# Two LSTM layers with attention and FFN on one core: bias written by VectorE, side work in equal steps, waits of the scan exchanged

## The reference

```python
def lstm(x, h0, Wx, Wh, b):            # c0 = 0
    for t in range(128):
        a = x[:, t] @ Wx + b + h @ Wh   # 16 x 512
        i, f, o, g = sigmoid(a_i), sigmoid(a_f), sigmoid(a_o), tanh(a_g)
        c = f * c + i * g
        h = o * tanh(c)
x = x + attention(lstm(x, cond, layer 1))   # linear attention scores, no softmax, scale 1/sqrt(128)
x = x + ffn(lstm(x, cond, layer 2))         # relu(h @ W1 + b1) @ W2 + b2, width 512
```

## Time and profile before

| | |
|---|---|
| runs, median (lowest to highest) | 485.77 us (484.74 to 487.51) |
| profiled execution, its own time | 481.0 us |
| its span, first to last instruction | 479.0 us |
| mean granted TensorE clock | 0.996 of 2.4 GHz |
| TensorE products busy | 462.4 us, 97% |
| TensorE weight loads busy | 349.3 us, 73% |
| VectorE busy | 260.7 us, 54% |
| ScalarE busy | 212.1 us, 44% |
| GpSimd busy | 17.4 us, 4% |
| DMA, mean over the span | 17 GB/s |

### The profile page before, as it was taken

How to read it: one execution, slowest core, us unless ns; L and a number is a source line. 1 busy time by engine, 2 the same in 40 slices (tenths; PEclk the granted TensorE clock), 3 DMA queues, 4 the chain that set the end, 5 groups by cost and what they waited for, 6 DMA issues and landing times.

```text
span 479.0 us, 17186 instructions
## 1 busy us (share of the span) xinstructions
PE 462.4 (97%) x6440; PEld 349.3 (73%) x6440; DVE 260.7 (54%) x1422; ACT 212.1 (44%) x1092; POOL 17.4 (4%) x29
## 2 busy tenths in 40 slices
PE   7999999999999999999999999999999999999997
PEld 5777666777666777766789877777777777777775
DVE  4545555555555555555545655555555555555554
ACT  2444444544444445444435344444444444444443
POOL 6700000000000000000000000000000000000000
PEclk9989999999999999999999999999999999999999
DMA  5010111110011111010000000000000000000000
GB/s 163 8 19 2 15 16 16 16 16 12 5 16 16 16 16 16 2 15 11 11 13 3 7 19 19 16 16 16 8 8 16 16 16 16 15 1 16 16 16 11
DMA packets 11689, 8.12 MB, mean 17 GB/s; under 512 B 1097, under 2 KB 11129, under 8 KB 11674
## 3 DMA queue, kind: packets, MB, share of 16 engines
q1 hardware_dynamic: 10874, 6.17, 6.5%
q0 software_dynamic: 512, 1.22, 0.9%
q10 hardware_dynamic: 288, 0.52, 0.3%
HBM read 2.87 MB, written 1.05 MB: 8 GB/s over the span
## 4 chain that ended last, share of the span: by engine, by line
PE 88%; DVE 4%; ACT 3%; issue 3%; DMA 1%; DVEq 0%; ACTq 0%
PE fobank L387 20%; PE gibank L377 16%; PE fobank L377 13%; PE bankV L363 5%; PE gibank L352 4%; PE bankY L531 4%; PE gibank L357 4%; PE fobank L352 4%; PE bankU L524 3%; PE fobank L357 3%; DVE cell L750 2%; PE bankV L441 2%; ACT scan L665 2%; PE bankU L459 2%; PE bankU L363 2%
## 5 line engine op out<-in xcount | busy, mean ns | idle before, releaser
L387 PEld LDWEIGHTS fobank<-ring,whf 128*128 128x128 f32 x510 | 76.5, 188 | 94.7 <-DVE ring L753 94.6
L662 ACT ACTIVATE fgate<-fobank 128x16 f32<-128x16 f32 x256 | 46.9, 183 | 164.8 <-PE fobank L387 162.5
L387 PE MATMUL fobank<-ring,whf 128*128 128x16 f32 x510 | 99.5, 270 | 10.4 <-DVE ring L753 0.7
L750 DVE TENSOR_TENSOR_SCAN cell<-scan 128x48 f32<-128x48 f32 x256 | 68.8, 269 | 53.2 <-ACT scan L665 52.8
L746 DVE TENSOR_TENSOR scan<-fgate,cell 128x16 f32<-128x16 f32 x256 | 45.3, 177 | 85.6 <-ACT fgate L662 83.7
L377 PEld LDWEIGHTS gibank<-h_hi,wh_parts 128*128 128x128 bf16 x1536 | 78.8, 110 | 0.0
L753 DVE SCALAR_TENSOR_TENSOR ring<-cell,ogate 128x16 f32<-128x16 f32 x256 | 44.7, 175 | 59.9 <-ACT cell L672 59.9
L377 PE MATMUL gibank<-h_hi,wh_parts 128*128 128x16 f16 x1536 | 75.4, 169 | 0.0
L377 PE MATMUL gibank<-h_lo,wh_parts 128*128 128x16 f16 x1536 | 75.3, 169 | 0.0
L665 ACT ACTIVATE scan<-gibank 128x32 f32<-128x32 f32 x256 | 54.8, 214 | 28.2 <-PE gibank L377 0.2
L377 PE MATMUL fobank<-h_hi,wh_parts 128*128 128x16 f16 x771 | 59.9, 174 | 0.4 <-ACT fgate L662 0.4
(11 more groups left out here) (150 smaller groups left out, 467.1 us busy)
## 6 DMA issues: line engine op xcount, KB each, us to landing
rows_t<-rows SPq DMA_DIRECT2D x16, 128.0 KB
x_rows<-in_x_dram SPq DMA_DIRECT2D x17, 64.0 KB
out_dram<-y_sb SPq DMA_DIRECT2D x16, 64.0 KB
xres<-x2T SPq DMA_DIRECT2D x15, 64.0 KB, 1.9
xin<-x2T SPq DMA_DIRECT2D x14, 64.0 KB, 1.8
w<-in_L_ffn_W_dram POOLq DMA_DIRECT2D x2, 256.0 KB, 3.9
wh<-in_L_cond_Wh_dram ACTq DMA_DIRECT2D x1, 256.0 KB, 2.8
wx<-in_L_cond_Wx_dram ACTq DMA_DIRECT2D x1, 256.0 KB, 3.9
```

The lines of the kernel that those rows point to most:

```text
L387: nc.tensor.matmul(step_out(p, t, GF), whf[layer][:], ring[:, (s - 1) % STEPS, :], start=False, stop=True, skip_group_check=True).then_inc ...
L662: nc.scalar.activation(fgate[:], fobank[p][:, NB * t:NB * t + NB], ACT.Sigmoid).then_inc(f_done[layer], 1)
L750: nc.vector.tensor_tensor_scan(out=c_scan, data0=scan_mul, data1=scan_add, initial=0.0, op0=ALU.mult, op1=ALU.add).then_inc(c_ready[layer], 1)
```

## The change

Six things:

1. The scan's two waits change places, and the f*c wait counts n + 1 instead of n + 2: the clearing of c has a semaphore of its own, waited for once per layer.
2. The bias matrices become 128 x 4 tiles, loaded element by element by two DMAs each (384 and 128 elements). `bias_gate` and the tile of ones are gone. VectorE writes the bias into the banks instead, by two broadcast copies of 256 elements per chunk, `seed_gi` and `seed_fo`; TensorE waits for both ahead of the chunk's first projection.
3. The copies stand behind steps t = 1, 2 (layer 1), t = 0, 1 (layer 2's loop), and together behind steps 1 and 11 of layer 2's first iteration, at the start, and between the layers.
4. Layer 1's row products move from t = 0 to t = 1; its projections from t = 2, 3 (one, three) to t = 3, 5 (two each). In layer 2's first iteration the four projections of step 12 move to 13, 14, 15 (one, one, two).
5. `WARM1` and `WARM2` are raised, and in layer 1 the filling passes go to `bankV` with a weight tile of zeros that adds to the bank, since it holds the early attention's sums.
6. The first four warming passes open the four gate banks instead.

```diff
-    WARM1 = [0, 0, 0, 0, 1, 3, 1, 3]
-    WARM2 = [1, 1, 0, 1, 1, 1, 1, 1]
+    WARM1 = [2, 1, 1, 1, 1, 1, 1, 3]
+    WARM2 = [1, 1, 1, 2, 1, 1, 2, 2]
...
-        bias = [sb(f"bias{n}", [P, 4 * H]) for n in (1, 2)]
+        bias = [sb(f"bias{n}", [P, 4]) for n in (1, 2)]
...
-            nc.vector.memset(c_psum, 0.0).then_inc(fc_done[layer], 1)
+            nc.vector.memset(c_psum, 0.0).then_inc(c_cleared, 1)
+            nc.vector.wait_ge(c_cleared, layer + 1)
+        def load_bias(eng, layer, b, done):
+            eng.dma_start(bias[layer][:, 1:4], b[0:3 * H].rearrange("(g p) -> p g", p=P),
+                          allow_slow_non_contiguous=True).then_inc(done, 16)
+            eng.dma_start(bias[layer][:, 0:1], b[3 * H:4 * H].unsqueeze(1),
+                          allow_slow_non_contiguous=True).then_inc(done, 16)
...
             sp.dma_start(x_rows[:, 0, :], x_ctb[0]).then_inc(rows_loaded[0], 16)
-            sp.wait_ge(bias1_cleared, 1)
-            sp.dma_start(bias[0][0:1, :], l1_b.unsqueeze(0)).then_inc(bias1_loaded, 16)
+            load_bias(sp, 0, l1_b, bias1_loaded)
...
+            def add_zeros(bank, n):
+                for _ in range(n):
+                    nc.tensor.matmul(bank[:, :], zeros[:, 0:P], warm_x[:], start=False, stop=True, skip_group_check=True)
...
-            keep_warm(bankV, 4)
+            for bank in (gibank[0], fobank[0], gibank[1], fobank[1]):
+                last = nc.tensor.matmul(bank[:, :], warm_w[:], warm_x[:], start=True, stop=True, skip_group_check=True)
+            last.then_inc(gate_banks_opened, 1)
...
-            pe.wait_ge(bias_ready, 1)
-            for g in GATES:
-                bias_gate(0, 0, g)
...
+            pe.wait_ge(seeded[0], 2)
             for g in GATES:
                 project_gate(0, 0, g, xT[:, 0, :])
...
+                    if t == 1:
                         pe.wait_ge(rows_kept, i * 2 + (p + 1))
                         row_products(1 - p, bankY)
-                    if t in (0, 1):
-                        for g in (GATES[0:1], GATES[1:])[t]:
-                            bias_gate(0, 1 - p, g)
...
+                    if t in (3, 5):
+                        if t == 3:
+                            pe.wait_ge(seeded[0], i * 4 + (2 * p + 4))
+                        rhs = xT[:, bass.ds(i * 2 + (p + 1), 1), :].rearrange("p c n -> p (c n)")
+                        for g in {3: GATES[0:2], 5: GATES[2:4]}[t]:
+                            project_gate(0, 1 - p, g, rhs)
...
-                    keep_warm(bankU, WARM1[t])
+                    add_zeros(bankV, WARM1[t])
...
-                    for g in GATES:
+                if s in (13, 14, 15):
+                    if s == 13:
+                        pe.wait_ge(seeded[1], 6)
+                    for g in {13: GATES[0:1], 14: GATES[1:2], 15: GATES[2:4]}[s]:
                         last = project_gate(1, 0, g, x2T[:, 2, :])
...
                         g = {2: GF, 3: GG, 6: GI, 7: GO}[t]
-                        bias_gate(1, 1 - p, g)
+                        if t == 2:
+                            pe.wait_ge(seeded[1], i * 4 + (2 * p + 4))
...
+            def seed_gi(layer, p):
+                nc.vector.tensor_copy(gibank[p][:, 0:2 * P].rearrange("p (t g b) -> p t g b", g=2, b=NB),
+                                      bias[layer][:, 0:2].unsqueeze(1).unsqueeze(3).broadcast_to([P, CH, 2, NB])
+                                      ).then_inc(seeded[layer], 1)
+            def seed_fo(layer, p):
+                nc.vector.tensor_copy(fobank[p][:, 0:2 * P].rearrange("p (g n) -> p g n", g=2),
+                                      bias[layer][:, 2:4].unsqueeze(2).broadcast_to([P, 2, P])
+                                      ).then_inc(seeded[layer], 1)
...
-                dve.wait_ge(fc_done[layer], n + 2)
                 dve.wait_ge(gi_done[layer], n1)
+                dve.wait_ge(fc_done[layer], n1)
```

More of the change, by code:

```diff
@@ L304, in _ @@
             pool.dma_start(wg_rows[:], w_g).then_inc(attn_w_loaded, 16)
-            nc.gpsimd.memset(bias[1][:], 0.0).then_inc(bias2_cleared, 1)
-            pool.wait_ge(bias2_cleared, 1)
-            pool.dma_start(bias[1][0:1, :], l2_b.unsqueeze(0)).then_inc(weights2_loaded, 16)
+            load_bias(pool, 1, l2_b, weights2_loaded)
             pool.dma_start(wx[1][:], l2_wx).then_inc(weights2_loaded, 16)
@@ L315, in _ @@
             nc.gpsimd.memset(x2T[:, NCH, :], 0.0).then_inc(set2_ready, 1)
-            pool.wait_ge(weights2_loaded, 112)
-            for w in (wx[1], wh[1], bias[1]):
-                nc.gpsimd.tensor_scalar(w[:, gate_cols(GG)], w[:, gate_cols(GG)], 2.0, None,
-                                        ALU.mult).then_inc(set2_ready, 1)
+            pool.wait_ge(weights2_loaded, 128)
+            for w in (wx[1][:, gate_cols(GG)], wh[1][:, gate_cols(GG)], bias[1][:, 0:1]):
+                nc.gpsimd.tensor_scalar(w, w, 2.0, None, ALU.mult).then_inc(set2_ready, 1)
             nc.gpsimd.tensor_scalar(w1[:], w1[:], 1.0 / H_UNIT, None, ALU.mult).then_inc(set2_ready, 1)
@@ L348, in moving @@
                 return tile if g in (GF, GO) else tile.rearrange("p (t b) -> p t b", b=NB)
-            def bias_gate(layer, p, g):
-                return nc.tensor.matmul(gate_out(p, g), bias[layer][:, gate_cols(g)], moving(ones[:, :], g),
-                                        start=g in (GF, GG), stop=False, skip_group_check=True)
             def project_gate(layer, p, g, tile):
@@ L544, in _ @@
                     score_products(P, hist[:, 0, :], P, P).then_inc(scores_ready, 1)
-                if s == 1:
-                    for g in GATES:
-                        bias_gate(1, 1, g)
                 if s == 2:
@@ L716, in _ @@
         def _(dve):
-            nc.vector.memset(bias[0][:], 0.0).then_inc(bias1_cleared, 1)
+            def seed_gi(layer, p):
[6 more added lines that the diff above has]
+                                      ).then_inc(seeded[layer], 1)
             nc.vector.memset(warm_w[:], 1.0)
             nc.vector.memset(warm_x[:], 1.0).then_inc(consts_ready, 1)
-            nc.vector.memset(ones[:], 1.0)
             nc.vector.memset(zeros[:], 0.0).then_inc(consts_ready, 1)
@@ L730, in _ @@
             start_h(0)
-            dve.wait_ge(bias1_loaded, 16)
-            nc.vector.tensor_scalar(bias[0][:, gate_cols(GG)], bias[0][:, gate_cols(GG)], 2.0, None,
-                                    ALU.mult).then_inc(bias_ready, 1)
+            dve.wait_ge(bias1_loaded, 32)
+            nc.vector.tensor_scalar(bias[0][:, 0:1], bias[0][:, 0:1], 2.0, None, ALU.mult).then_inc(bias_ready, 1)
+            dve.wait_ge(gate_banks_opened, 1)
+            dve.wait_ge(bias_ready, 1)
+            seed_gi(0, 0)
+            seed_fo(0, 0)
             dve.wait_ge(wh1_loaded, 16)
@@ L775, in _ @@
                     p, t = s // CH, s % CH
+                    if t == 1:
+                        seed_gi(0, 1 - p)
+                    if t == 2:
+                        seed_fo(0, 1 - p)
                     if t == 5:
@@ L837, in _ @@
                     c = i * 2 + p
+                    if t == 0:
+                        seed_gi(1, 1 - p)
+                    if t == 1:
+                        seed_fo(1, 1 - p)
                     if t == 2:
```

29 lines of the change are left out of this document (16 added, 13 removed).

## The result

The changed kernel takes 472.12 us (median of 4 runs, 470.36 to 500.24) against 486.64 (484.74 to 490.51) for the kernel before on the same chip: ratio 0.968, 95% interval 0.960 to 0.976, so faster. The forecast was 468.5 with a range to 476.0. The profiled execution took 472.32 with a span of 470.0, where the forecast for a profile was 463.7. The medians are 14.5 apart where 17.3 was forecast; the profiled executions, whose own times are 481.0 and 472.3, are 8.7 apart. So the direction holds, and in the profiles, where the sum was made, half of the gain is missing.

A forecast was written before the change was run, and what follows sets the result against it. The prediction took a chain handed from engine to engine each time step as the bound. Gains of 16.0 (loops and first iteration), 0.76 (layer 2's first sixteen steps) and 0.5 (start) sum to 17.26: 485.77 to 468.5 us, range 464.5 to 476.

The forecast's parts named there:

- Swapped waits: Scan in each time step: with the gate-tanh wait riding on it, 0.067 us gained per step, 16.0 over 239 steps.
- The 0.045 in hand on the other path: f*c path to the scan: with its separate wait it is still in time, by some 0.045 us.
- TensorE's room: TensorE side work per step: a unit is 0.24 us; four overrun the shorter step by 0.07, three fit; no loop cost.
- Copies: Bias copies on VectorE, two per chunk: 350 ns each, hidden in 0.54 us of room, so zero cost singly.
- That rival: VectorE bias copies cost more than their 0.54 us room; at 0.65 each, 6.6 us comes back, total 475; chance 0.07.
- Layer 2's first sixteen steps: Written-out start of layer 2: waits gain only partly, bias units leave TensorE, paired copies cost; net 0.76 us gained.
- nothing is gained by the removed products as such, since they were under cover: TensorE side work: taking bias products away saves no time in itself, because they ran hidden under the chain.
- The fourth rival: Loop steps: TensorE's clock falls to 1.2 GHz, 0.49 us per step; 64 such steps give 499.5; chance 0.07.
- Between the layers: Up to layer 2's first state: four bias products leave TensorE, two copies enter VectorE; taken as 0, 0.5 either way.
- Start: Before the first projection: bias products leave, copies and element-wise bias loads come; 0.5 us gained, ends 1.5 either way.
- the 4.8 between median and profile: Whole kernel: unprofiled median 485.77 lies 4.8 us above the profiled execution; the gain was taken as the same in both.
- late loads: Start: the bias fetched by 4-byte elements lands 3 us later than the b1 row says, total 471; chance 0.06.

The follow-up runs named there:

- the kernel whose first state came at 11.79: The changed kernel with layer 1's loop stripped of its zero-adding passes (WARM1 all zero): 503.93 us, ratio 1.044 against the kernel before.

## Why the prediction was right, and where it was wrong

**Swapped waits: right in size, half in cause.** 239 steps at 0.067 is what the loops show (1.771 to 1.704; in the kernel with the waits alone to 1.700). The rule taken from the earlier trace rows, that the wait written first rides on the scan, holds only if nothing stands between. It held here because the change also took away the arithmetic of n + 2. The change's first item lists that count, but the prediction's working gives it no part, so this was luck: by its own account the exchange alone should have given 16 us, and it gave none. The 0.045 in hand on the other path held. One remark fits: the Trainium skill (Perfetto Trace Analysis, Identifying Dependency Chains) says that instructions waiting on several engines may have event-semaphore instructions inserted before them for the additional waits. The traces agree, x256 at 21 ns, and add which of the two waits is inserted and what it costs.

**TensorE's room: mis-sized, harmless.** "With the step 0.067 shorter four would stand over by 0.07": measured, nothing for four and 0.20 for five. The error is in the size of a unit: 0.24 divided the whole time up to the forget-gate load by four, and that load was waiting for the state. In the kernel with the waits alone the same four leave room for the load after 0.89, so a unit is at most 0.22.

**Copies: right.** 420 ns in place of 350, inside the room of 0.54; a pair costs 0.11 to 0.12 for 0.08, although the copies are longer than taken, as they overlap by 0.09. That rival is out.

**Layer 2's first sixteen steps: the step that failed.** "Steps 8 to 11 lose three bias units that stood on TensorE's path, 0.72" and the rest of the net 0.76 was a sum over room alone, at an assumed full clock. Measured: 3.8 lost in place of 0.76 gained (39.87 against 36.09). With the clock held by fills the stretch takes 35.89, 0.2 gained, with the fills standing where the bias products stood; with the waits alone 35.76. The bias units were worth less than forecast even where the changed kernel's clock was full: the three steps behind 8, 9 and 10 took 6.98 against 7.40, 0.42 less. Likewise "nothing is gained by the removed products as such, since they were under cover": true of the time on the path and wrong for the clock, where work under cover did count. The fourth rival had the right mechanism, but I looked for it in the loops, which the change refills, and not where it takes bias products away without refilling.

**Between the layers: right.** 5.49 against 5.52 for the interval up to layer 2's first state.

**Start: wrong sign.** 0.5 gained was forecast; the first state came 0.2 later, and with the first iteration, which should have gained another 1.0, 0.5 was lost. The loads were judged too darkly: the bias came 0.56 later, where 1.6 was allowed for, and the projection 1.22 earlier, where 0.5 was forecast. The Trainium skill (DMA: Bandwidth & Descriptors, Rules for kernel authors) warns of a last dimension that is not contiguous; the trace agrees in direction, by these 0.56. What decided was the clock: its rise at 20.7 in place of 9.8 takes back what the start had won, as the kernel whose first state came at 11.79 shows. Why it rises later is open.

**A stall that was not foreseen.** In seven of layer 1's loop iterations (all but the first) the step that follows t = 3 of the first chunk takes 1.78 to 1.79, which makes 0.6. The gate tanh is on time there and the scan starts 0.08 later, at the same place of the loop every time. Every kernel with the copies has such a longer step there, the one with the waits alone has none. Its cause is open.

Together: start and first iteration 2.0, layer 2's first iteration 4.5, loops 1.8 make 8.3 of the 8.6 between 463.7 and 472.3; the other 0.3 lies outside the span.

**The median: nearer than its working deserved.** It missed by 3.6 where the profile missed by 8.6. The prediction carried the 4.8 between median and profile over to the new kernel; there the median, 472.12, lies at the profile, 472.32, while the kernel before measured 486.64 beside its 481.0. And the range went up to 476 for dear copies and late loads, neither of which came; a clock that falls for a short time was not in it. That the median fell inside is luck in this part; the gain itself, 14.5 of 17.3, is not.

## What to carry to other kernels

Where the last signal on a chain arrives through the second of two waits, make it the one that rides on the instruction, and look at what the queue holds between: a count computed in a loop puts a register instruction there that takes the wait. Before removing work that hides under something else, look at each stretch it leaves for what keeps the clock; the loops may be refilled and the written-out first iterations not. And run the smallest part alone first: here the two waits and one semaphore gave everything, and with the rest of the change the profiled span was 8.1 longer (470.0 against 461.9; the two were not run against each other on one chip).

## What was not expected of the hardware

- A register instruction of 40 ns that stands between a wait and the scan takes the wait's place ahead of it: the gap from signal to scan is then 0.13, against 0.10 with a separate wait and 0.04 with the wait on the scan itself.
- The granted clock's first rise differed widely between kernels whose first instructions are the same: 20.7 in the changed kernel, 68.5 and 91.0 in two that differ from it only later or by the place of one copy. Three-unit steps at 1.2 GHz (2.33) can go on for tens of microseconds. The Trainium skill (TensorE: Matmul & The Clock Gate, Part 1) says that the number of slow products at the start varies between runs of one kernel. The profiles here, one for each kernel, agree in kind, but more widely: of three kernels with the same instructions up to the end of layer 1 two rose at 20.7 and 23.1, the third at 68.5.
- The page's clock row shows full speed until the first recorded change. Only the durations tell the start's level (1.20 against 0.68 for one 256-column product).
